# A decoder layer on one core: other places for fills, sums, evacuations and shared units, and no products of zeros in the cross attention

## The chip, the cores and the metric

One core of one Trainium2 chip runs the whole layer in one launch. The metric is the device time of that launch in microseconds (us); before the change the median of three runs is 1231.83, from 1230.77 to 1233.53. The engines are TensorE (PE, with PEld for its weight loads), VectorE (DVE), ScalarE (ACT), GpSimd (POOL) and SyncE (SP), which issues most of the transfers. All arithmetic is in float32.

## The reference

Eight sequences of 100 tokens, 512 wide, pass through one layer. Each of its three parts is added to its input, and each reads a layer norm of it:

```python
x = x + attn(layernorm(x))            # 16 query heads, 4 key heads, rotary, values 128 wide
x = x + xattn(layernorm(x), ctx)      # 16 heads of 32; ctx has 345 tokens and 16 more (DCA)
x = x + ffn(layernorm(x))             # 60 experts of 352, 4 per token, and a shared one of 1408

# xattn: queries and keys are normed per head
q = ln(x @ Wq + bq);  k = ln(y_main @ Wk + bk);  v = y_main @ Wv + bv
k_dca, v_dca = ln(y_dca @ Wk_dca + ...), y_dca @ Wv_dca + ...
ctx = softmax(q k^T) v + softmax(q k_dca^T) v_dca
return ctx @ Wo + bo
# ffn: silu(x @ gate.T) * (x @ up.T) @ down.T for the shared expert and for the four chosen ones
```

## The kernel before

The sequences are taken in four **pairs** (j = 0 and 1 in each). Before the first pair a **preamble** loads weights, centres some of them, and projects the first sequence's context, three chunks of 115 tokens, to keys and values (`FIRST_BANKS`, L783 on TensorE, L1619 and L1621 on VectorE). It also makes the keys of the 16 DCA tokens: VectorE norms them (L1609), TensorE transposes them (L788), ScalarE scales them (L1279, signal `kd_ready`).

Each engine then runs a loop over the pairs in an order that is written out by hand. A PSUM bank is handed on by semaphores: `attention_fills` lists which product fills which of the eight banks and in which order; `begin` (in `project` and the transposes) waits until the bank's former content is evacuated, `end` tells that it is full, `wait_filled` and `wait_drained` are the other side. A fill that is listed in another bank or at another place waits for another evacuation.

A pair begins with the self attention (L818 to L906). In its second half are the **ten steps** of the cross attention, `for t in range(STEPS)`: a step takes four heads of one sequence, steps 0 to 3 those of j = 0 and 4 to 7 those of j = 1, and works on three groups at once. TensorE forms the scores of group t (`four_scores`, L954, banks 0 to 3), multiplies the probabilities of group t - 2 with the values (`four_values`, L972), and transposes the probabilities of group t - 1 in three parts (`four_transposes`, L963, banks 4 and 5). VectorE takes the four maxima (`four_max`, L1771) and copies the three transposed parts (`four_T`, L1775), ScalarE does the exponentials (`four_exp`, L1340). Between them stands other work that has to be done some time:

- `STEP_HOOKS` names for each step the products that TensorE forms between the second and the third transposes, in bank 7 (6 from step 6): projections of context chunks to keys and values (`kx`, `vx`, L824; VectorE evacuates them, L1698 and L1702), the query projection `xq` and its transposes `xqT` (L842, after a norm on GpSimd, L687 to L704), the scores of the DCA tokens `ds` (L920), the transposes of their probabilities `dpT` (L928), the spread of the softmax sums `rx` (L994, from `spread_sums` on ScalarE) and the output projection `xo`.
- `STEP_ZEROS` says how often `keep_busy` multiplies zeros by zeros (L983, 128x200) before and after the third transposes. They are added to the open accumulation of the context and change nothing in it. Step 0 has two more.
- On VectorE `few(n)` puts in pieces of layer norms: in steps 1 to 4 that of the next pair's x, in steps 7 and 8 that of the third norm. `sums(j)` forms the reciprocal sums, `dca_softmax` the DCA softmax in three pieces, `residual` adds `xo` to x.

SP issues its transfers strictly in order. After the weights it writes zeros to the buffers of the routed tokens, `fill_zeros` with L464, 29 MB in nine pieces; then it enters the loop over pairs and loads the next pair's context (L430) and x (L427).

Behind the last pair the **shared expert** runs in 22 units, `shared_up(u)` (L1105): unit u is block `m = u // 2` of hidden columns for half of the tokens, `half = u % 2`. The tokens come back from DRAM transposed (`xT3`): six sequences early, the last two when the last pair is done (`xT3_loaded`). A unit from 3 on waits for the hidden product of the unit three before it (`sh_h`, L1976 on VectorE), which needs ScalarE's `silu` (L1426). Beside the units VectorE chooses experts (L1890 to L1905), whose ranks TensorE forms before unit 5 (`RANK_AT`, L1136). The routed experts follow, whose weights are loaded once the units are done.

## Time and profile before

| | us |
|---|---|
| median of three runs | 1231.83 (1230.77 to 1233.53) |
| the profiled execution | 1232.9 |
| its span, first to last instruction | 1231.1 |
| pair 0 on TensorE | from 42.08 |
| pair 1 | from 196.78, its ten steps from 271.39 to 339.51 |
| end of pair 3, first shared unit | 639.89 |
| first routed rows | 773.88 |

### The profile page before, as it was taken

What the parts mean: (1) busy time and instruction counts of PE and PEld (TensorE: products, weight loads), DVE (VectorE), ACT (ScalarE), POOL (GpSimd) and SP (SyncE); (2) the same over time, 40 slices, a digit from 0 to 9 for tenths busy, and PEclk for the clock granted to TensorE, in tenths of its full rate; (3) what the DMA queues carried; (4) which work ended last, traced back from release to release, by engine and by line L of the source; (5) the groups of instructions that cost most, each with busy time, mean ns of one, the idle gap of its engine ahead of it and who ended that gap; (6) DMA issues with size and microseconds to landing.
All of it is one profiled execution on the core that took longest, in us unless ns stands there. A gap on an engine that the chain in (4) does not pass through costs nothing.

```text
span 1231.1 us, 18953 instructions
## 1 busy us (share of the span) xinstructions
PE 1113.6 (90%) x5566; PEld 601.4 (49%) x5566; DVE 503.9 (41%) x1385; ACT 259.8 (21%) x804; POOL 369.3 (30%) x843
## 2 busy tenths in 40 slices
PE   3799889998899989999888999998888899898998
PEld 1444555445554455544554655454444445444454
DVE  7634665348554374535655711221111111121144
ACT  0142322323333332323313000111111011011100
POOL 3385451756337471574100171000000000000172
PEclk9899899999899999999998999999899899899999
DMA  8999101000010000102006592899999999999653
GB/s 313 347 397 375 36 2 54 14 12 2 2 54 14 13 1 22 39 8 92 1 27 168 178 345 75 288 383 383 383 384 380 375 385 389 388 383 381 224 139 114
DMA packets 76580, 233.06 MB, mean 189 GB/s; under 512 B 11362, under 2 KB 13766, under 8 KB 68814
## 3 DMA queue, kind: packets, MB, share of 16 engines
q1 hardware_dynamic: 58830, 197.90, 44.4%
q10 hardware_dynamic: 11520, 20.98, 4.7%
q0 software_dynamic: 6144, 13.13, 3.6%
q8 instruction: 42, 0.69, 0.2%
q14 instruction: 44, 0.36, 0.1%
HBM read 178.75 MB, written 53.22 MB: 188 GB/s over the span
## 4 chain that ended last, share of the span: by engine, by line
PE 38%; DMA 9%; issue 2%; SPq 2%; DVE 1%; ACT 0%; DVEq 0%; ACTq 0%
PE ps L1105 10%; DMA arena<-in_w 8%; PE ps L1172 7%; PE ps L1168 5%; PE ps L1266 5%; PE ps L1203 3%; PE ps L1199 3%; PE ps L824 1%; PE ps L1160 1%; PE ps L1187 1%; SPq L537 1%; PE ps L963 0%; SPq L538 0%; SPq L539 0%; PE ps L983 0%
## 5 line engine op out<-in xcount | busy, mean ns | idle before, releaser
L824 PE MATMUL ps<-arena 128*100 128x512 f32 (+3 forms) x576 | 230.3, 548 | 15.0 <-DVE arena L1742 5.5
L761 POOL DMA_INDIRECT arena<-ys_d,slot_u x32 | 36.7, 1145 | 429.6 <-issue 427.1
L824 PEld LDWEIGHTS ps<-arena 128*100 128x100 f32 (+1 forms) x576 | 88.5, 176 | 113.3 <-issue 95.9
L1172 PE MATMUL ps<-arena 128*64 128x352 f32 x640 | 115.1, 519 | 30.4 <-issue 16.2
L1105 PE MATMUL ps<-arena 128*128 128x400 f32 x352 | 122.0, 509 | 6.9 <-DMA arena<-xT_d 6.0
L1991 DVE COPY arena<-ps 128x512 f32<-128x512 f32 x40 | 27.7, 692 | 234.1 <-PE ps L1160 234.1
L906 PE MATMUL ps<-arena 128*100 128x512 f32 x256 | 114.1, 593 | 0.0
L1168 PE MATMUL ps<-arena 128*128 128x352 f32 x320 | 98.0, 459 | 0.8 <-issue 0.8
L1105 PEld LDWEIGHTS ps<-arena 128*128 128x128 f32 x352 | 67.8, 194 | 59.6 <-issue 8.7
L1340 ACT ACTIVATE arena<-ps,arena 100x345 f32<-100x345 f32 x128 | 69.4, 546 | 123.3 <-DVE arena L1771 120.4
L1172 PEld LDWEIGHTS ps<-arena 128*64 128x64 f32 x640 | 52.9, 154 | 84.9 <-issue 67.4
L687 POOL TENSOR_TENSOR arena<-arena 115x512 f32<-115x512 f32 (+1 forms) x29 | 30.2, 1041 | 181.0 <-DVE arena L1698 145.5
L1168 PEld LDWEIGHTS ps<-arena 128*128 128x128 f32 x320 | 59.2, 190 | 30.7 <-issue 1.0
L906 PEld LDWEIGHTS ps<-arena 128*100 128x100 f32 x256 | 42.3, 166 | 62.2 <-issue 58.8
L749 POOL DMA_INDIRECT xs_d<-arena,slot_u x32 | 32.7, 1022 | 124.7 <-DVE slot_u L1957 115.2
L1771 DVE TENSOR_REDUCE arena<-ps 100x1 f32<-100x345 f32 x128 | 61.9, 508 | 17.3 <-PE ps L954 17.3
L1444 ACT ACTIVATE arena<-ps 128x352 f32<-128x352 f32 x40 | 18.6, 464 | 238.1 <-PE ps L1172 145.2
L1266 PE MATMUL ps<-arena 128*128 128x400 f32 x176 | 59.5, 500 | 2.0 <-issue 2.0
L1775 DVE COPY arena<-ps 115x400 f32<-115x400 f32 x92 | 52.4, 570 | 21.5 <-PE ps L963 21.3
L963 PEld LDWEIGHTS ps<-ident,arena 100*115 100x115 f32 x384 | 49.4, 191 | 20.6 <-issue 19.6
L1203 PE MATMUL ps<-arena 128*64 128x512 f32 (+1 forms) x240 | 56.0, 601 | 0.7 <-DVE arena L2007 0.7
L690 POOL TENSOR_TENSOR arena<-arena 115x256 f32<-115x256 f32 (+3 forms) x116 | 53.5, 461 | 9.1
(222 smaller groups left out, 1488.1 us busy)
## 6 DMA issues: line engine op xcount, KB each, us to landing
arena<-in_w SPq DMA_DIRECT2D x60, 1408.0 KB, 12.4
arena<-in_w SPq DMA_DIRECT2D x60, 512.0 KB, 13.0
xs_d<-zero SPq DMA_DIRECT2D x5, 3328.0 KB, 25.5
arena<-in_w SPq DMA_DIRECT2D x60, 192.0 KB, 14.0
arena<-xs_d ACTq DMA_DIRECT2D x40, 256.0 KB, 8.0
ys_d<-arena ACTq DMA_DIRECT2D x40, 256.0 KB, 7.6
ys_d<-zero SPq DMA_DIRECT2D x2, 3328.0 KB, 24.6
arena<-in_se_up SPq DMA_DIRECT2D x11, 512.0 KB, 6.5
```

The source lines that it names most:

```text
L690: then(nc.gpsimd.tensor_tensor(s3[:, :, 0:w], s3[:, :, 0:w], s3[:, :, w:2 * w], ALU.add))
L824: last = nc.tensor.matmul(ps[0:m, k, 0:cols[1] - cols[0]], lhs(c), w[:, c, cols[0]:cols[1]], start=(c == 0), stop=(c == n_c - 1))
L906: last = nc.tensor.matmul(ps[0:S, j, :], cT[c % 2][:, g, :], w_out[:, c * G + g, :], start=(c == 0 and g == 0), stop=(c == KV - 1 and g == ...
L963: last = nc.tensor.transpose(ps[0:LC, k, r * S:(r + 1) * S], xp[(4 * t + r) % NP_][0:S, c * LC:(c + 1) * LC], ident[0:S, 0:S])
L1105: last = nc.tensor.matmul(ps[:, (u % 3) * 2 + gu, 0:400].rearrange("p (a b) -> p a b", a=4), se_w[m % 3][:, c, gu * P:(gu + 1) * P], tok, ...
L1168: last = nc.tensor.matmul(ps[:, 1 + gu, 0:I], xsT[0][:, c, :], w13_s[s][0][:, c, at:at + I], start=(c == 0), stop=(c == DC - 1))
L1172: last = nc.tensor.matmul(ps[half * HALF:(half + 1) * HALF, 3 + gu, 0:I], xsT[1][:, c, half * HALF:(half + 1) * HALF], w13_s[s][1 + half][ ...
L1203: last = nc.tensor.matmul(ps[half * HALF:(half + 1) * HALF, 7, :], hT[1][0:w, n, half * HALF:(half + 1) * HALF], w2_s[s][1 + half][0:w, n, :],
L1266: last = nc.tensor.matmul(ps[:, half * 4 + d, 0:400], w_down[:, m, d * P:(d + 1) * P], hT_all[:, m, half * 400:(half + 1) * 400], start=(m ...
L1340: nc.scalar.activation(xp[(4 * t + r) % NP_][0:S, :], ps[0:S, k, 0:LM], ACT.Exp, bias=xnm[0:S, j, h:h + 1], scale=1.0, accum_out=xsum[0:S, ...
L1771: nc.vector.tensor_reduce(xnm[0:S, j, h:h + 1], ps[0:S, k, 0:LM], AX, ALU.max, negate=True).then_inc(xmax_ready.sem, 1)
L1775: nc.vector.tensor_copy(xpT[0:LC, c, :], ps[0:LC, k, 0:4 * S]).then_inc(free[k].sem, 1)
```

## The change

Seven things are done, all in the order of the work; the products that remain are the same.

1. All products of zeros in the steps go (`STEP_ZEROS` is zero throughout, and the two in step 0 are deleted).
2. Hooks can now also stand ahead of the first transposes (`HEAD_HOOKS`) and behind the third (`TAIL_HOOKS`). `rx` of j = 0 goes to the head of step 5. `xqT` and the last key chunk go to the tail of step 3, the first value chunk to the tail of step 5, the second `dpT` to that of step 8. Banks change with them.
3. ScalarE spreads the sums of j = 0 after step 4 instead of inside step 5, and copies `rx` and `dpT` out in the other order. VectorE adds the residual `xo` of j = 0 after two maxima of step 7 instead of after four.
4. In the preamble the banks of the first projections change, the last one follows the transposes of the DCA keys, VectorE waits for `kd_ready` only behind its work on the chunks, and pair 0 starts when the first chunk is evacuated.
5. The context of pair 1 is loaded ahead of the zero fills.
6. In later pairs the next context is loaded after the last value chunk, which is now in bank 2.
7. The shared units run in the order of `UP_ORDER`: three blocks for the first half of the tokens, then these for the second half, then block by block; units 1 and 2 stand ahead of the wait for the last tokens.

```diff
+UP_ORDER = [(m, half) for half in range(2) for m in range(3)] + [(m, half) for m in range(3, MC) for half in range(2)]
...
-STEP_HOOKS = {1: [("xq", 1)], 2: [("kx", 0, 1)], 3: [("xqT", 1)], 4: [("kx", 0, 2), ("ds", 1)],
-              5: [("dpT", 0), ("rx", 0), ("vx", 0, 0)], 6: [("xo", 0)], 7: [("vx", 0, 1)], 8: [("dpT", 1)]}
-STEP_ZEROS = {1: (0, 0), 2: (0, 2), 3: (2, 3), 4: (0, 2), 5: (0, 2), 6: (0, 2), 7: (0, 2), 8: (2, 0)}
+HEAD_HOOKS = {5: [("rx", 0)]}
+STEP_HOOKS = {1: [("xq", 1)], 2: [("kx", 0, 1)], 4: [("ds", 1)], 5: [("dpT", 0)], 6: [("xo", 0)], 7: [("vx", 0, 1)]}
+TAIL_HOOKS = {3: [(("xqT", 1), 7), (("kx", 0, 2), 4)], 5: [(("vx", 0, 0), 7)], 8: [(("dpT", 1), 3), (("vx", 0, 2), 2)]}
+STEP_ZEROS = {t: (0, 0) for t in range(1, 9)}
...
-    out += [(("rx", 1), 6), (("xT3", 0), 6), (("gate", 0), 6), (("xo", 1), 0)]
+    out += [(("rx", 1), 1), (("xT3", 0), 6), (("gate", 0), 3), (("xo", 1), 0)]
...
-        FIRST_BANKS = ((2, 3, 5), (6, 7, 0))
+        FIRST_BANKS = ((2, 6, 3), (5, 7, 1))
...
             sp.dma_start(w_gate, gates.rearrange("(c p) n -> p c n", p=P)).then_inc(w_loaded["w_gate"], 16)
 
+            sp.wait_ge(first_full, 2 * LN_)
+            load_context(1, 0)
+
             sp.wait_ge(pool_pre, 7)
...
-                    sp.wait_ge(sh_up, 2 * (m - 3) + 2)
+                    sp.wait_ge(sh_up, UP_ORDER.index((m - 3, 1)) + 1)
...
-                sp.wait_ge(first_full, 2 * LN_)
-                sp.wait_ge(full[6].sem, full[6].before(i))
-                load_context(min(i + 1, PAIRS - 1), 0)
+                if i:
+                    sp.wait_ge(full[2].sem, full[2].before(i))
+                    load_context(min(i + 1, PAIRS - 1), 0)
...
             for c in range(LN_):
...
+                first_project(0, c)
+                if c < LN_ - 1:
+                    first_project(1, c)
             pe.wait_ge(dca_n, 3)
...
             last.then_inc(dca_t, 1)
+            first_project(1, LN_ - 1)
             pe.wait_ge(kd_ready, 1)
             pe.wait_ge(w_loaded["w_attn"], 16)
-            pe.wait_ge(first_free, 2 * LN_)
+            pe.wait_ge(first_free, 2)
...
+                    if j == 0:
+                        pe.wait_ge(first_free, 2 * LN_)
                     project(("k", j), S, rows, w_attn, (D, QK), DC)
...
                         transpose_x("xT2", 2, 1)
-                        keep_busy(0, 2)
...
+                    for key in HEAD_HOOKS.get(t, []):
+                        hooks[key[0]](*key[1:])
                     if 1 <= t <= FOURS:
                         four_transposes(t - 1, 0)
...
-                    if t == FOURS:
-                        context_project("vx", 0, 2)
+                    for key, _ in TAIL_HOOKS.get(t, []):
+                        hooks[key[0]](*key[1:])
...
-                m, half = u // 2, u % 2
+                m, half = UP_ORDER[u]
...
+            for u in range(1, 3):
+                shared_up(u)
             pe.wait_ge(xT3_loaded, 16 * 2)
-            for u in range(1, RANK_AT):
+            for u in range(3, RANK_AT):
                 shared_up(u)
...
                         if (t, r) == (5, 0):
-                            spread_sums(0)
-                        if (t, r) == (5, 1):
+                            spread(0)
+                        if (t, r) == (5, 2):
                             dca_T(0)
-                        if (t, r) == (5, 2):
-                            spread(0)
...
+                    if t == 4:
+                        spread_sums(0)
...
             dve.wait_ge(dca_n, 3)
-            dve.wait_ge(kd_ready, 1)
             for c in range(LN_):
...
+                    if t == 7:
+                        residual("xo", 0)
                     few(1)
...
                     if t == 7:
-                        residual("xo", 0)
                         run(pieces)
...
                     four_T(t - 1, 2)
+                    for key, _ in TAIL_HOOKS.get(t, []):
+                        if key[0] in ("kx", "vx"):
+                            (context_key if key[0] == "kx" else context_value)(*key[1:])
                     few(2)
```

Three places in the built programs show it. First SP's queue, in the preamble: what it issues after the values of the DCA tokens. Before:

```order
L457 DMA arena<-in_Wo 128x4x512
L458 DMA arena<-in_gates 128x4x61
L464 DMA xs_d<-zero 128x13x512 [waits pool_preamble]
L464 DMA xs_d<-zero 128x13x512 x4
L464 DMA xs_d<-zero 128x11x512
L464 DMA ys_d<-zero 128x13x512 x2
```

and now:

```order
L459 DMA arena<-in_Wo 128x4x512
L460 DMA arena<-in_gates 128x4x61
L432 DMA arena<-in_ctxT 128x690 [waits first_context_full]
L469 DMA xs_d<-zero 128x13x512 [waits pool_preamble]
L469 DMA xs_d<-zero 128x13x512 x4
L469 DMA xs_d<-zero 128x11x512
```

The load of the next context moved from behind all fills to ahead of them; the load of the next x stays behind.

Second TensorE in step 3, from the wait for the normed queries to the end of the step. L802 (now L810) and L419 (L421) only wait, `bank5_free` is the evacuation of bank 5. Before:

```order
L802 REGISTER_ALU [waits heads_normed]
L842 MATMUL ps<-ident,arena 128x100 [waits bank7_free]
L842 MATMUL ps<-ident,arena 128x100 x3
L983 MATMUL ps<-zero 128x200 x2
L802 REGISTER_ALU
L963 MATMUL ps<-ident,arena 115x100 [waits bank5_free]
L963 MATMUL ps<-ident,arena 115x100 x3
L983 MATMUL ps<-zero 128x200 x3
```

and now:

```order
L973 MATMUL ps<-ident,arena 115x100 [waits bank5_free]
L973 MATMUL ps<-ident,arena 115x100 x3
L810 REGISTER_ALU [waits heads_normed]
L850 MATMUL ps<-ident,arena 128x100 [waits bank7_free]
L850 MATMUL ps<-ident,arena 128x100 x3
L832 MATMUL ps<-arena 115x512 [waits bank4_free]
L832 MATMUL ps<-arena 115x512
```

The third transposes (L963, now L973) moved ahead of the transposed queries (L842, now L850), the zeros are gone, and the last key chunk (L832) came from step 4.

Third TensorE in step 5, from the second transposes on. Before:

```order
L963 MATMUL ps<-ident,arena 115x100 [waits bank4_free]
L963 MATMUL ps<-ident,arena 115x100 x3
L802 REGISTER_ALU [waits dca_probs_ready]
L928 MATMUL ps<-ident,arena 128x100 [waits bank7_free]
L928 MATMUL ps<-ident,arena 128x100
L802 REGISTER_ALU [waits spread_sums_ready]
L994 MATMUL ps<-ident,arena 128x100 [waits bank7_free]
L994 MATMUL ps<-ident,arena 128x100 x3
L802 REGISTER_ALU
L824 MATMUL ps<-arena 115x512 [waits bank7_free]
L824 MATMUL ps<-arena 115x512
```

and now, from the products with the values of group 3 on:

```order
L982 MATMUL ps<-arena 32x100 x3
L810 REGISTER_ALU [waits spread_sums_ready]
L1004 MATMUL ps<-ident,arena 128x100 [waits bank7_free]
L1004 MATMUL ps<-ident,arena 128x100 x3
L973 MATMUL ps<-ident,arena 115x100 [waits bank3_free,bank2_free,bank5_free,bank1_free,bank0_free]
L973 MATMUL ps<-ident,arena 115x100 x3
L973 MATMUL ps<-ident,arena 115x100 [waits bank4_free]
L973 MATMUL ps<-ident,arena 115x100 x3
L810 REGISTER_ALU [waits dca_probs_ready]
L938 MATMUL ps<-ident,arena 128x100 [waits bank7_free]
```

The spread of the sums (L994, now L1004) moved from behind `dpT` (L928, now L938) to ahead of the first transposes; the value chunk (L824) now follows the third ones.

## Rows read from the trace of the kernel before

**Rows 1.** The page: share of TensorE, and one of its costliest groups (ScalarE).

```profile
PE 1113.6 (90%) x5566; PEld 601.4 (49%) x5566; DVE 503.9 (41%) x1385; ACT 259.8 (21%) x804; POOL 369.3 (30%) x843
...
L1340 ACT ACTIVATE arena<-ps,arena 100x345 f32<-100x345 f32 x128 | 69.4, 546 | 123.3 <-DVE arena L1771 120.4
```

**Rows 2.** Groups by form, TensorE: count | busy us, mean ns | idle before.

```profile
L983 PE MATMUL ps<-zero 128*128 128x200 f32 x152 | 35.8, 364 | 0.0
```

**Rows 3.** Timeline of TensorE in the steps of pair 1.

```profile
276.71 0.86 PE L983 MATMUL ps<-zero 128*128 128x200 f32 x4
...
293.19 0.56 PE L842 MATMUL ps<-ident,arena 100*128 100x100 f32 x4 [1.44 <-POOL arena L704]
...
295.67 1.88 PE L983 MATMUL ps<-zero 128*128 128x200 f32 x6
...
299.79 1.89 PE L824 MATMUL ps<-arena 128*115 128x512 f32 x4
...
308.89 0.56 PE L994 MATMUL ps<-ident,arena 100*128 100x100 f32 x4 [1.80 <-ACT arena L1303]
310.05 3.17 PE L824 MATMUL ps<-arena 128*115 128x512 f32 x4 [0.59 <-ACT arena L1303]
...
315.60 0.84 PE L954 MATMUL ps<-arena 32*100 32x345 f32 x8
...
323.39 0.84 PE L954 MATMUL ps<-arena 32*100 32x345 f32 x8
...
327.24 3.29 PE L824 MATMUL ps<-arena 128*115 128x512 f32 x4 [1.37 <-DVE arena L1742]
```

**Rows 4.** Timeline of VectorE in the steps of pair 1.

```profile
282.80 0.69 DVE L1707 TENSOR_TENSOR arena<-ps,arena 100x512 f32<-100x512 f32 x1 [0.70 <-PE ps L824]
...
292.65 0.56 DVE L1775 COPY arena<-ps 115x400 f32<-115x400 f32 x1
...
295.91 0.57 DVE L1775 COPY arena<-ps 115x400 f32<-115x400 f32 x1 [0.84 <-PE ps L963]
...
298.33 0.94 DVE L1771 TENSOR_REDUCE arena<-ps 100x1 f32<-100x345 f32 x2 [1.59 <-PE ps L954]
...
302.33 1.04 DVE L1544 TENSOR_TENSOR arena<-arena 100x1 f32<-100x1 f32 x1
...
306.38 1.35 DVE L1771 TENSOR_REDUCE arena<-ps 100x1 f32<-100x345 f32 x3
...
316.45 0.94 DVE L1771 TENSOR_REDUCE arena<-ps 100x1 f32<-100x345 f32 x2 [1.87 <-PE ps L954]
```

**Rows 5.** Busy time by stretch, the ten steps of pair 1; behind POOL the granted clock.

```profile
271.39:339.51 68.12, 60.58 (x483) 38.15 (x483) 48.34 (x139) 23.86 (x75) 31.34 (x89) 0.92 0.02 7
```

**Rows 6.** Timeline of VectorE, preamble and step 1 of pair 0.

```profile
36.99 0.69 DVE L1619 TENSOR_TENSOR arena<-ps,arena 115x512 f32<-115x512 f32 x1 [3.75 <-ACT arena L1279]
...
132.37 0.68 DVE L1553 BATCH_NORM_STATS2 arena<-arena 100x6 f32<-100x512 f32 x1
```

**Rows 7.** Timeline of TensorE, start of pair 0 and its step 0.

```profile
42.08 1.59 PE L818 MATMUL ps<-ident,arena 100*128 100x100 f32 x8 [6.72 <-DVEq L1622]
...
125.96 3.38 PE L824 MATMUL ps<-arena 128*115 128x512 f32 x4 [3.42 <-DMA arena<-in_ctxT]
```

**Rows 8.** Timeline of SP's queue, pair 0: last fills and the context behind them.

```profile
84.04 24.64 SPq L464 DMA_DIRECT2D ys_d<-zero  x3
108.80 6.62 SPq L430 DMA_DIRECT2D arena<-in_ctxT  x1
```

**Rows 9.** Timeline of ScalarE, step 5 of pair 1.

```profile
308.51 0.33 ACT L1303 ACTIVATE arena<-ps 128x200 f32<-128x200 f32 x1
```

**Rows 10.** Timeline of TensorE, the first shared units.

```profile
639.89 5.64 PE L1105 MATMUL ps<-arena 128*128 128x400 f32 x16 [0.87 <-DVE arena L1742]
...
653.37 24.44 PE L1105 MATMUL ps<-arena 128*128 128x400 f32 x64 [5.98 <-DMA arena<-xT_d]
```

**Rows 11.** Timeline of VectorE, its first hidden product of the shared units.

```profile
663.87 0.57 DVE L1976 TENSOR_TENSOR arena<-arena,ps 128x400 f32<-128x400 f32 x1 [2.96 <-ACT arena L1426]
```

25 lines of the change are left out of this document (12 added, 13 removed).

## The prediction, made before the changed kernel ran

> **What bounds the kernel now.** I read the page first: TensorE is busy for 90% of the span [rows 1], so time on its path is what counts. The groups by form then show products of `zero` alone [rows 2]: 76 matmuls (each is two records), 35.8 us, in steps 0 to 8 of the cross attention, 19 in each pair. They can go, but the time follows only where TensorE itself is late. So I read TensorE's instructions of pair 1 in order of time [rows 3]: the largest stalls in its ten steps are 1.44 (for the norm of queries on GpSimd), 1.80 and 0.59 (for ScalarE's copies out of bank 7) and 1.37 (for VectorE's residual); with three of 0.8 they come to 7.5 us. VectorE in the same stretch [rows 4] has no wait between those at 282.80 and 295.91, so steps 2 and 3 are its own. Last comes the clock [rows 5]: the steps take 68.1 us at a mean of 0.92. The loss stands in [rows 3]: a projection of keys takes 1.89, but 3.17 and 3.29 behind the stalls, not far from the half rate of 1.2 GHz. Of 68.1 us some 47 are work at full clock: less 7.5 of stalls, 8.2 of zeros (19 at 0.43, as two take 0.86 [rows 3]) and 5.4 that the clock takes (8%).
>
> **The head.** VectorE stands 3.75 us for ScalarE's keys of the short context before it touches the first chunks [rows 6], and TensorE stands 6.72 until all six are evacuated [rows 7]. Now VectorE begins 3.75 earlier and pair 0 asks for the first chunk alone, so it starts between 3.75 and 6.72 earlier. The context for pair 1, 345 KB, goes out ahead of the zero fills, so the wait of 3.42 and the slow projection behind it (3.38 for 1.89) [rows 7] go as well. That adds up to some 9 to 12 us, 11 with a start 6 earlier, but I do not count it. SP is shut in the fills until 108.80 [rows 8], and the next x is still behind them: with the context moved ahead the same bytes stand in front of it. The context landed at 125.96 [rows 7]; I take 126.3 for x. VectorE started the norm that needs it at 132.37 [rows 6]. So the head gives 6.0, and the rest turns into a wait for x; between 5 and 7, as x lands at 127.4 or 125.4.
>
> **Steps 0 to 3.** The zeros ahead of step 1 go, so the query projection is evacuated 0.8 earlier (VectorE waited 0.70 for it [rows 4]), and its unbroken chain moves by that. TensorE, with no zeros, comes to the third transposes of step 3 at about 290.3 and stands some 2.0 us for the copy that before starts at 292.65 [rows 4]: longer than the 1.44 that it replaces. Behind it stand the transposed queries and now also the last key chunk, moved here from step 4, which VectorE must evacuate before its first maximum of step 4. At full clock that maximum comes at 296.5 instead of 298.33 [rows 4], 1.8 less; with the chunk at half the clock (3.4 instead of 1.7), 0.2 less. I take 0.7, nearer the slow end: behind the stall of 1.44 three products of zeros took 1.88, where two took 0.86 before [rows 3].
>
> **Steps 4 and 5.** From that maximum to the first of step 6 it is 18.1 us before (298.33 to 316.45 [rows 4]). Step 4 on VectorE, 8.05 to 306.38, loses the evacuation of the key chunk (0.7), the waits around it (0.6) and most of an instruction of 1.04 that takes 0.16 elsewhere (0.7) [rows 4]: 6.05. The spread of the sums (`rx`) moves ahead of the transposes, but its bank 7 is free only when VectorE has read the scores of the short context at that step's end: TensorE stands 1.9 us there, in place of the 1.80 later on. Then a maximum and an exponential (0.5 and 0.6 [rows 1]), the spread's copy (0.5), two exponentials (1.1) and the `dpT` copy (0.33 [rows 9]) free bank 7 for the value chunk: 3.1. Chunk 1.8, products of the short context 1.0, first scores 0.3: 12.3 in all, 5.8 less. If the clock falls behind the stall, the chunk and what stands around it take up to 2.3 longer: 3.5 less. I take 4.8, as the work between stall and chunk uses up most of a slow stretch.
>
> **Step 6** runs without a stall from 315.60 to 323.39 [rows 3]; only its zeros go: 0.9 (0.8 to 0.9).
>
> **Steps 7 to 9** take 16.1 us before (323.39 [rows 3] to the end at 339.51 [rows 5]). The residual now follows the second maximum, so the wait of 1.37 goes, and the slow chunk of 3.29 with it. VectorE then bounds them. By [rows 4] two maxima take 0.9, a copy 0.5, an evacuation 0.7, a piece of a norm 0.2: counted from the scores, first maximum at 1.0, residual done at 2.5, maximum, copy and maximum to 3.9, pieces and second copy to 5.2, chunk 5.8, third copy 6.7, sums 8.05, next copy 8.6. TensorE stands 1.6 for the third copy and 0.75 for the last; its chunk and spread end at 11.3, the norm that the next transposes need at 13.5: 13.6, so 2.5 less. With the last chunk at half the clock 0.8 less. I take 1.1, near the slow end, for two stalls close together.
>
> **Shared units.** Units 1 and 2 now need the early tokens alone and fill the stall of 5.98 ahead of 653.37 [rows 10]. But unit 3 waits for the first hidden product, which VectorE starts at 663.87, late itself behind router and activation tables [rows 11]. With 5.5 a unit [rows 10] TensorE stands from 658.4 to 664.5 and begins slowly, as it does now: four units took 24.44 where 22 would do. Unit 4 ends at about 677.6 either way: 0, between 2.2 less (no slow start) and 0.5 more. The later weight loads wait for unit 3 instead of 1, but two more units and the ranks stand ahead of their use. Everything behind is shifted whole.
>
> **Sum.** A pair saves 0.7 + 4.8 + 0.9 + 1.1 = 7.5 (5.3 to 11.0), four of them 30, the head 6: 36.0 less. The profiled execution took 1232.9 us, so 1196.9; the median is 1.1 lower: **1196**. The bounds together: 7 + 44 + 2.2 less gives 1179, 5 + 21.2 - 0.5 gives 1206.
>
> **Rivals.** (1) *Slower: the clock.* The zeros hold the engine busy; without them the steps could run by turns at 1.2 and 2.4 GHz. With half of the 47 us at 1.2 GHz the work takes 70.5, and with some 5 of stalls 7.4 more than 68.1; four pairs less the head make 24 more, 1256; with no stalls left 1236. It decides once more than 27% of the work runs slow: 47 x 1.27 and 10 of stalls are 68.1 plus the 1.5 of head for each pair. For it: the slow projections of pair 1 stand behind stalls of 1.4 to 2.4 us, and I expect new ones of 1.6 to 2.0. Against: slow stretches ended while TensorE had work, and slow work fills stalls. Chance 0.08.
> The Trainium skill, "TensorE: Matmul & The Clock Gate", section "A second HAM failure mode: psum-queue depth-cycling", says that short idle times between groups of matmuls, as PSUM banks are cycled, can make the clock swing between its levels; it speaks against this change, and by it the time would be this rival's. The trace agrees that it happens (a mean of 0.92 [rows 5]), not that it goes on.
> (2) *Small gain.* Each stall brings a slow stretch that falls on the chunk VectorE waits for, and the head gives less: 2 to 5 a pair, 1207 to 1223, around 1214. Chance 0.14.
> (3) *x lands early.* Then the head gives its 11: 1191. Against it: the context, right ahead of x in the queue, came at 125.96 [rows 7]. Chance 0.10.
> (4) *Nothing measurable.* Zeros and moves only change places with stalls, within 0.2% (2.5 us, about what a measurement can tell): 0.03.
> My forecast has 0.65.
>
> **Range and chances.** 1178 to 1212 holds the forecast's bounds, rival 3 and a third of rival 2. Faster 0.65 + 0.10 + 0.14 = 0.89, same 0.03, slower 0.08.
>
> **What would show it.** No products of zeros by 200 columns. Pair 0 starts 4 to 6 us earlier, and VectorE waits for x until about 126. The steps take near 60 us, with stalls of about 2 us ahead of the third transposes of step 3 and ahead of the spread in step 5, both for VectorE, and none for GpSimd's norm. From the end of the last pair to the ranks the distance is unchanged, with a stall of about 6 us ahead of unit 3. The mean clock of the steps tells the rivals apart: 0.85 to 0.93 is mine, under 0.8 the first. I am wrong if the steps shrink by more than 11 or less than 5 us, or if x does not hold pair 0.

## The result, and the profile after

The changed kernel takes 1221.74 us (median of 20 runs, 1209.33 to 1233.12) beside 1229.34 for the kernel before (20 runs, 1223.70 to 1234.19). The ratio is 0.9915, 95% interval 0.9892 to 0.9938. It counts the 14 runs that lie within 1.5% of the fastest, while the medians of all 20 give 0.9938. Measured a second time the changed kernel took 1228.23 beside 1230.65, a ratio of 0.9977 (0.9947 to 1.0007). So by the medians it is 7.6 and 2.4 us faster, and the second interval takes in no difference as well; 36 were forecast, and both medians lie above the forecast's range of 1178 to 1212. The first profiled execution was the longest of those 20 runs; the rows below are from one of the second measurement, 1223.36 us (span 1221.5).

TensorE's busy share has not moved against [rows 1]; the page says:

```profile
PE 1099.5 (90%) x5414; PEld 583.7 (48%) x5414; DVE 505.9 (41%) x1385; ACT 260.8 (21%) x804; POOL 368.1 (30%) x843
```

The busy time by stretch (columns as in [rows 5]; behind the granted clock stand the busy share of the DMA engines and what they moved, in GB/s): self attention of pair 0; its steps up to pair 1; the ten steps of pair 1; from the first routed products to the end.

```profile
36.40:113.01 76.61, 74.24 (x328) 36.73 (x328) 37.02 (x92) 23.53 (x88) 49.93 (x119) 1.00 1.04 376
113.01:191.65 78.64, 65.35 (x466) 36.44 (x465) 49.07 (x140) 24.89 (x77) 31.00 (x89) 0.85 0.21 70
...
266.32:330.35 64.03, 56.25 (x445) 33.41 (x444) 48.43 (x139) 24.16 (x75) 31.30 (x89) 0.89 0.03 7
...
756.40:1221.40 465.00, 418.62 (x1804) 218.33 (x1804) 101.09 (x239) 46.45 (x88) 34.07 (x32) 0.95 0.91 327
```

The steps of pair 1 take 64.0 us instead of 68.1 [rows 5], at a granted clock of 0.89 instead of 0.92; pair 0 from its steps on runs at 0.85. Where the slow work lies is seen in the timeline of TensorE in pair 1, which answers to [rows 3] (a transpose shows as one record, so x12 in L973 are twelve):

```profile
287.55 1.09 PE L973 MATMUL ps<-ident,arena 100*115 100x100 f32 x4 [1.84 <-DVE arena L1788]
288.43 0.87 PE L850 MATMUL ps<-ident,arena 100*128 100x100 f32 x4
289.10 2.79 PE L832 MATMUL ps<-arena 128*115 128x512 f32 x4
...
300.37 0.56 PE L1004 MATMUL ps<-ident,arena 100*128 100x100 f32 x4 [1.84 <-DVE arena L1764]
...
303.15 2.65 PE L832 MATMUL ps<-arena 128*115 128x512 f32 x4
...
306.60 0.84 PE L964 MATMUL ps<-arena 32*100 32x345 f32 x8
...
313.69 0.84 PE L964 MATMUL ps<-arena 32*100 32x345 f32 x8
...
316.76 1.97 PE L832 MATMUL ps<-arena 128*115 128x512 f32 x4 [0.60 <-DVE arena L1755]
...
320.97 0.38 PE L982 MATMUL ps<-arena 115*32 115x100 f32 x8 [1.01 <-DVE arena L1788]
321.52 2.73 PE L973 MATMUL ps<-ident,arena 100*115 100x100 f32 x12 [0.17 <-issue]
324.05 0.54 PE L938 MATMUL ps<-ident,arena 100*128 100x100 f32 x2
324.38 3.65 PE L832 MATMUL ps<-arena 128*115 128x512 f32 x4
327.82 0.82 PE L1004 MATMUL ps<-ident,arena 100*128 100x100 f32 x4
...
330.70 0.56 PE L826 MATMUL ps<-ident,arena 100*128 100x100 f32 x4 [0.35 <-DVE arena L1577]
```

The predicted stalls are there: 1.84 ahead of the third transposes of step 3 and 1.84 ahead of the spread in step 5, both for VectorE. Behind each the next chunk is slow: 2.79 and 2.65, where one at full clock takes 1.89 [rows 3]. The worst comes in step 8. Stalls of 0.60 (in step 7) and 1.01 (in step 8) come first, and all of step 8 from its transposes on runs at half the clock: its chunk takes 3.65.

VectorE in the same pair, which answers to [rows 4]: first maximum of step 4, two small instructions of step 4's norm, first maximum of step 6.

```profile
292.94 0.94 DVE L1784 TENSOR_REDUCE arena<-ps 100x1 f32<-100x345 f32 x2
...
296.02 0.60 DVE L1557 TENSOR_TENSOR arena<-arena 100x1 f32<-100x1 f32 x1
296.66 0.96 DVE L1560 SCALAR_TENSOR_TENSOR arena<-arena 100x1 f32<-100x1 f32 x1
...
307.46 0.94 DVE L1784 TENSOR_REDUCE arena<-ps 100x1 f32<-100x345 f32 x2 [0.93 <-PE ps L964]
```

In pair 0 VectorE now stands for x, and TensorE behind it; the answer to [rows 6], and TensorE's row:

```profile
126.73 0.69 DVE L1566 BATCH_NORM_STATS2 arena<-arena 100x6 f32<-100x512 f32 x1 [6.10 <-DMA arena<-in_x]
...
128.38 1.10 PE L973 MATMUL ps<-ident,arena 100*115 100x100 f32 x4 [4.69 <-DVE arena L1788]
```

The queue of SP, which answers to [rows 8], shows why x comes then: SP issues it only when it gets out of the three fills of the results.

```profile
84.77 24.74 SPq L469 DMA_DIRECT2D ys_d<-zero  x3
109.63 8.47 SPq L429 DMA_DIRECT2D arena<-in_x  x2
```

Pair by pair, from the first transposes of x to those of the next pair: pair 0 now 155.3 (154.7 before), though it starts 5.7 earlier; pair 1 144.6 (148.1); pair 2 143.4 (147.5). The first routed products start at 756.40 instead of 775.37, 19.0 earlier. From there to the end, in what is called the routed stretch below, it is 465.1 us instead of 455.8, with the same code: 9.3 are gone again. In the first profiled execution, the one of 1233.12 us, the first routed products started at 761.70, 13.7 earlier than before, and the stretch took 469.7.

### The profile page after: what moved, and what is told of

The parts are those of the page before. It is cut to its first block, busy times and chain, and to the rows that moved or that the text cites. A ratio compares the mean times of both kernels' runs of the same rounds, so it can differ in the third digit from the quotient of the medians.

```text
span 1231.3 us, 18523 instructions
## 1 busy us (share of the span) xinstructions
PE 1107.0 (90%) x5414; PEld 588.4 (48%) x5414; DVE 506.1 (41%) x1385; ACT 261.5 (21%) x804; POOL 372.9 (30%) x843
## 4 chain that ended last, share of the span: by engine, by line
PE 64%; DMA 12%; SPq 8%; DVE 8%; issue 6%; ACT 1%; DVEq 0%; ACTq 0%
PE ps L832 14%; DMA arena<-in_w 9%; PE ps L1116 9%; PE ps L916 7%; PE ps L1185 7%; PE ps L1181 5%; SPq L469 5%; PE ps L1279 5%; PE ps L1216 3%; PE ps L1212 3%; PE ps L973 2%; PE ps L905 1%; DMA arena<-in_x 1%; DVE arena L1784 1%; DVE arena L1788 1%
## 5 line engine op out<-in xcount | busy, mean ns | idle before, releaser
L832 PE MATMUL ps<-arena 128*100 128x512 f32 (+3 forms) x576 | 233.3, 553 | 7.6 <-ACT arena L1301 3.7
L1185 PE MATMUL ps<-arena 128*64 128x352 f32 x640 | 119.6, 535 | 39.6 <-issue 31.9
L832 PEld LDWEIGHTS ps<-arena 128*100 128x100 f32 (+1 forms) x576 | 91.1, 181 | 107.3 <-issue 95.4
L1185 PEld LDWEIGHTS ps<-arena 128*64 128x64 f32 x640 | 56.5, 158 | 95.2 <-issue 70.1
L1116 PEld LDWEIGHTS ps<-arena 128*128 128x128 f32 x352 | 67.7, 194 | 60.1 <-issue 9.1
L1181 PEld LDWEIGHTS ps<-arena 128*128 128x128 f32 x320 | 59.2, 190 | 30.7 <-issue 1.0
L973 PE MATMUL ps<-ident,arena 100*115 100x100 f32 x384 | 59.3, 297 | 16.0 <-DVE arena L1788 15.4
L973 PEld LDWEIGHTS ps<-ident,arena 100*115 100x115 f32 x384 | 51.1, 202 | 32.1 <-DVE arena L1788 19.5
```

What stands on the lines that cost most here:

```text
L832: last = nc.tensor.matmul(ps[0:m, k, 0:cols[1] - cols[0]], lhs(c), w[:, c, cols[0]:cols[1]], start=(c == 0), stop=(c == n_c - 1))
L973: last = nc.tensor.transpose(ps[0:LC, k, r * S:(r + 1) * S], xp[(4 * t + r) % NP_][0:S, c * LC:(c + 1) * LC], ident[0:S, 0:S])
L1116: last = nc.tensor.matmul(ps[:, (u % 3) * 2 + gu, 0:400].rearrange("p (a b) -> p a b", a=4), se_w[m % 3][:, c, gu * P:(gu + 1) * P], tok, ...
L1181: last = nc.tensor.matmul(ps[:, 1 + gu, 0:I], xsT[0][:, c, :], w13_s[s][0][:, c, at:at + I], start=(c == 0), stop=(c == DC - 1))
L1185: last = nc.tensor.matmul(ps[half * HALF:(half + 1) * HALF, 3 + gu, 0:I], xsT[1][:, c, half * HALF:(half + 1) * HALF], w13_s[s][1 + half][ ...
```

## The experiments

### The clock: zeros back, zeros alone, zeros only in the stalls

**after_again, before_again.** Both kernels once more, unchanged, for the spread of their stretches.

> The changed kernel once more. Two things of its first profile are in question: the routed experts took 471.1 us from their first weights to the end (457.2 before), and the pairs gained 2 to 4 us each. If the transfer rate of the routed weights differs from execution to execution, with no tie to the change, that stretch is anything between 445 and 470 here, longer where its rate in GB/s is lower. If starting it earlier makes it longer, it is 471 within 3 again. The pairs should repeat within 2 us each: pair 1 144.6, pair 2 145.7, pair 3 138.7 from the first transposes of x to those of the next pair.

> The kernel before once more, for the spread of its stretches: if the transfer rate of the routed weights varies from execution to execution, its routed stretch is not 455.8 us at 383 GB/s again but anywhere from 450 to 465, longer at a lower rate; the pairs repeat to 1 us (148, 147.5, 142).

Measured: the changed kernel 1228.23 us (10 runs), pairs 1 and 2 at 144.6 and 143.4, routed stretch 465.1 at 375 GB/s. The kernel before in a single run 1225.94, pairs 1 and 2 at 147.2 and 146.8, stretch 447.9 at 392 GB/s (455.8 at 383 in the first profile). The stretch moves with its transfer rate.

The pairs repeat less well than expected: pairs 1 and 2 to within 2.4 us, but pair 3 of the changed kernel, from its first transposes to the ranks, took 182.2 in the first profile and 179.1 in the second, and pair 0 of the kernel before 154.7 and 157.7. before_padded and before_light (below) run the code of the kernel before up to the routed experts too, and after_light that of the changed one. By the means of these four and three executions the change gains 0.9 us in pair 0, 2.8 in pair 1 and 2.5 in pair 2, and the first routed products start 16.6 earlier (from 774.3 to 776.2 before, from 756.4 to 761.7 now). The first profile of the kernel before, by which the prediction was made, has the shortest pair 0 and the longest pairs 1 and 2 of its four.

**all_zeros** (the diff is against the changed kernel, as below where nothing else is said):

```
-STEP_ZEROS = {t: (0, 0) for t in range(1, 9)}
+STEP_ZEROS = {1: (0, 0), 2: (0, 2), 3: (2, 3), 4: (0, 2), 5: (0, 2), 6: (0, 2), 7: (0, 2), 8: (2, 0)}
...
                         transpose_x("xT2", 2, 1)
+                        keep_busy(0, 2)
```

> The changed kernel with all 19 products of zeros a pair put back where they stood, two of them in step 0. Theory A (the clock): without them TensorE falls to half its clock behind each stall, and the work behind it pays. Then step 8 of pair 1 runs at the full clock (12 transposes 1.6 us instead of 2.74, the last value chunk 1.9 instead of 3.65), steps 7 to 9 take 15 instead of 17.0; against that stand up to 0.43 for each of the zeros that does not fall into a stall, some 10 of them, 4 a pair: time the same within 0.5%, granted clock of the ten steps 0.93 to 0.97 instead of 0.89. Theory B (VectorE bounds the steps, the clock of TensorE only fills its waits): the zeros cost their 8.2 us a pair less what lies in stalls (4), so 4 us a pair, 16 in all, 1.3% slower than the changed kernel, equal to the kernel before or slower.

Measured: 1218.44 us, 0.9916 of before (0.9886 to 0.9946), where the kernel without zeros had 0.9977 on the same chip and 0.9915 in the first measurement: the time does not tell the two apart, the steps have to. The steps of pair 1 take 63.5 us, at a clock of 0.95. Step 8 in TensorE's timeline:

```profile
320.24 0.38 PE L982 MATMUL ps<-arena 115*32 115x100 f32 x8 [0.66 <-DVE arena L1789]
320.75 1.02 PE L973 MATMUL ps<-ident,arena 100*115 100x100 f32 x8
321.61 0.87 PE L993 MATMUL ps<-zero 128*128 128x200 f32 x4
322.31 0.55 PE L973 MATMUL ps<-ident,arena 100*115 100x100 f32 x4
322.70 0.34 PE L938 MATMUL ps<-ident,arena 100*128 100x100 f32 x2
322.88 1.90 PE L832 MATMUL ps<-arena 128*115 128x512 f32 x4
```

The chunk takes 1.90 instead of 3.65. Theory A holds for the steps, theory B (16 us slower) falls: 19 products of zeros a pair cost nothing, the first routed products even start 1.9 us earlier (754.5) than in after_again. The rest of the difference between the two profiles lies in the routed stretch, 452.1 us at 389 GB/s in this one.

**stall_zeros:**

```
-STEP_ZEROS = {t: (0, 0) for t in range(1, 9)}
+STEP_ZEROS = {t: (0, 0) for t in range(1, 9)} | {3: (4, 0), 4: (0, 2), 7: (0, 2)}
...
+                    if t == 5:
+                        keep_busy(0, 4)
                     for key in HEAD_HOOKS.get(t, []):
```

> The changed kernel with 12 products of zeros a pair, only where TensorE stands: 4 ahead of the third transposes of step 3 (1.85 us of waiting), 2 at the end of step 4 (0.93), 4 ahead of the spread in step 5 (1.84), 2 at the end of step 7 (1.01). Theory A (the clock): the chunks of keys and values behind them take 1.9 instead of 2.6 to 3.65, step 8 runs at the full clock; 0.7 in step 3, 0.7 in step 5, 1.5 to 3 in steps 7 to 9: 3 to 4.5 a pair, 12 to 18 us in all, 0.978 to 0.982 of the kernel before. Theory B (VectorE bounds the steps): the zeros lie in waits and change nothing, time that of the changed kernel within 0.3%.

Measured: 1214.06 us, 0.9863 of before (0.9799 to 0.9926; 4 runs), the steps of pairs 1 to 3 at 60.8, 60.9 and 59.2 us, clock 0.97. Step 3 of pair 1:

```profile
281.74 1.54 PE L993 MATMUL ps<-zero 128*128 128x200 f32 x8
283.74 0.65 PE L973 MATMUL ps<-ident,arena 100*115 100x100 f32 x4 [0.47 <-DVE arena L1790]
284.23 0.51 PE L850 MATMUL ps<-ident,arena 100*128 100x100 f32 x4
284.96 1.97 PE L832 MATMUL ps<-arena 128*115 128x512 f32 x4 [0.23 <-DVE arena L1790]
```

The zeros lie in the stall and cost nothing; the chunk takes 1.97 instead of 2.79. The steps gain 3.8, 3.2, 1.9 and 1.2 us in pairs 0 to 3 against after_again: theory A, at two thirds of the size forecast. Two places are left. In step 5 of pair 1 a stall of 1.12 remained behind the zeros, and the value chunk still took 3.62. And behind the steps of pairs 1 and 2 the clock falls now: between them and the next pair it is 0.78, where it was 1.00 in after_again, and the projections there take 6.05 in pair 1, where they took 4.36 in the kernel before. First the two rows of step 5, then the projections here and in the kernel before:

```profile
295.33 0.56 PE L1004 MATMUL ps<-ident,arena 100*128 100x100 f32 x4 [1.12 <-DVE arena L1766]
...
298.11 3.62 PE L832 MATMUL ps<-arena 128*115 128x512 f32 x4 [0.37 <-ACT arena L1318]
...
325.10 6.05 PE L832 MATMUL ps<-arena 128*100 128x61 f32 x16 [0.59 <-ACT arena L1303]
```

```profile
340.71 4.36 PE L824 MATMUL ps<-arena 128*100 128x61 f32 x16 [0.69 <-ACT arena L1288]
```

So counted from pair to pair the gain is only 3.1, 1.5 and 0.2 us in pairs 0 to 2, and the first routed products start 4.7 earlier than in after_again (751.70), not 10.

**before_no_zeros** (against the kernel before): both lines of all_zeros the other way round.

> The kernel before with its products of zeros left out and nothing moved: the zeros alone. Theory A (the clock): the 8.2 us of zeros a pair kept the clock up; where VectorE and ScalarE are waited for anyway, the stalls grow and more of the chunks run at half the clock: 0 to 2 us a pair less than before, 0 to 0.7% faster, clock of the ten steps 0.86 to 0.90. Theory B (TensorE simply had 8.2 us too much to do): 4 to 5 us a pair less, 1.3 to 1.6% faster.

Measured: 0.9996 of before (0.9964 to 1.0028), no difference. In the profile the first routed products start 6.7 us earlier; the steps of pair 1 take 65.6 us, 2.7 less, at a clock of 0.92, though steps 4 and 5 take 20.6 from scores to scores where they took 18.1. That lies between the theories; three other executions with the code of the kernel before took 66.0 to 67.3, and against those it is 0.4 to 1.7 less, which agrees with A, as the time does.

The kernels together, ten steps of pairs 1, 2 and 3 (from the first scores to the end of the last product of the short context):

| kernel | zeros a pair | steps, us | clock, pair 1 |
|---|---|---|---|
| before | 19 | 68.3 67.7 66.7 | 0.93 |
| before_no_zeros | 0 | 65.6 64.8 63.8 | 0.92 |
| all_zeros (moves alone) | 19 | 63.5 62.5 59.2 | 0.95 |
| changed (after_again) | 0 | 64.0 62.8 60.5 | 0.89 |
| stall_zeros | 12 | 60.8 60.9 59.2 | 0.97 |
| stall_zeros_early_x | 14 | 59.1 59.1 59.8 | 1.00 |

By this table, with the old order, taking the zeros out saves 2.8 us in the steps of a pair; with the moves made, it costs 0.7; the moves themselves save 5.8. One row is one execution, and those of one kernel differ: over the three pairs the changed kernel took 64.2 us a pair on average in its first profile and 62.4 in the second. By the means of the four executions of the kernel before and the three of the changed one the figures are 2.2, 1.3 and 5.2. So the moves clearly shorten the steps, and the cost of leaving all zeros out is small beside that spread.

### The head: what holds x

**early_x:**

```
-            fills_started += fill_zeros(ys_d, TILES, TILES + NOV)
-            assert fills_started == ZERO_FILLS
...
                     load_context(i + 1, 1)
+                    if i == 0:
+                        fills_started += fill_zeros(ys_d, TILES, TILES + NOV)
+                        assert fills_started == ZERO_FILLS
```

> The changed kernel with the three zero fills of the results (9.2 MB) put behind the loads of x and of the second context, nothing else: the order of SP's queue alone. Theory X (the fills in flight hold x): x lands some 10 us earlier, TensorE's wait of 6.4 us in pair 0 goes with the slow clock behind it, pair 0 is 7 to 10 us shorter than 79.0, the other pairs stay as they are (144.6, 145.7, 138.7); 7 to 10 us less than the changed kernel. The rest of the gain of the combined kernel over that with the zeros in the stalls alone then comes from the two more products of zeros. Rival: the gain came from those zeros, pair 0 stays within 2 us.

Measured: 1214.26 us, 0.9895 of before (0.9866 to 0.9925). SP's queue:

```profile
43.81 41.31 SPq L469 DMA_DIRECT2D xs_d<-zero  x6
85.24 8.13 SPq L429 DMA_DIRECT2D arena<-in_x  x2
115.73 0.36 SPq L432 DMA_DIRECT2D arena<-in_ctxT  x1
116.13 12.80 SPq L469 DMA_DIRECT2D ys_d<-zero  x3
```

x goes out 24 us earlier, right behind the fills ahead of it, so its own waits were over by then, and pair 0 takes 144.9 us instead of 155.3: 10.4 less, with pairs 1 and 2 as they were (144.1, 143.8). Theory X holds, a little above its upper end; the time is 7.5 and 14.0 us under the two medians of the changed kernel.

**stall_zeros_early_x:** both diffs in one, with `keep_busy(0, 6)` in step 5.

> The kernel with zeros in the stalls (4 in step 3, 2 in step 4, here 6 ahead of the spread of step 5, 2 in step 7) and, in pair 0, the three zero fills of the results (9.2 MB) put behind the loads of x and of the second context. If the fills in flight hold x, it lands at about 115 to 118 instead of 127.5, TensorE's wait of 6.4 us for VectorE's copy goes and the slow clock behind it: pair 0 is 6 to 10 us shorter than 79.0. If x has another cause (its own wait for the first residual at 111), less than 2. The 2 more products of zeros in step 5 cover the wait of 1.12 that was left there and bring the value chunk of 3.62 to 1.9: 1 to 2 us in pairs 1 and 2. Together 7 to 13 us less than with the zeros in the stalls alone, which is 0.973 to 0.981 of before.

Measured: **1195.31 us (1194.1 to 1196.4, 4 runs), 0.9712 of before (0.9679 to 0.9745)**, faster than both kernels, a little better than expected. The value chunk of step 5 in pair 1, with the zeros, the stall that is left, and the granted clock of the ten steps by stretch:

```profile
281.89 2.30 PE L994 MATMUL ps<-zero 128*128 128x200 f32 x12
284.65 0.56 PE L1005 MATMUL ps<-ident,arena 100*128 100x100 f32 x4 [0.46 <-DVE arena L1767]
...
287.43 1.97 PE L833 MATMUL ps<-arena 128*115 128x512 f32 x4 [0.38 <-ACT arena L1319]
```

```profile
251.87:310.98 59.11, 54.92 (x473) 33.70 (x472) 47.97 (x139) 24.18 (x75) 31.50 (x89) 1.00 0.03 8
```

early_x is the same kernel without the 14 products of zeros, and that makes it the clearest test of them: 1214.26 us without, 1195.31 with them, and the intervals against before do not touch. Of the 20.0 us between the two profiles 13.2 come ahead of the routed experts (746.77 and 733.60), where the clock in the steps of pair 1 is 0.89 and 1.00; the rest lies in the routed stretch, at 375 and 381 GB/s.

### The shared units

**units_undone:** `UP_ORDER` plain, all units but the first behind `xT3_loaded`.

> The changed kernel with the shared units in their old order and the wait for the last tokens ahead of unit 1 again. Theory of the prediction: the order is worth nothing, as the wait only moves to the first hidden product; from the end of the last pair to the ranks 43 to 44 us, as with it (43.47) and before (42.98). Rival: the new order is worth one of the two waits, 2 us or more. If it also had a part in the slower routed stretch of the changed kernel, the median would fall by 8.

Measured: 1224.66 us (1221.05 to 1228.53). From the last product of the steps to the ranks 43.96 us, with the new order 43.95. It is worth nothing, as predicted.

### The routed stretch: what takes 9 us back

**after_light, before_light.** From the third round on SP loads only the down weights:

```
+            def reload(s, b, at):
...
+                rows = w2[e, 0:256, :].rearrange("(p c) n -> p c n", c=2)
+                for c in range(2):
+                    sp.dma_start(w2_s[s][b][:, c:c + 1, :], rows[:, c:c + 1, :]).then_inc(w_ready[s][b], 16)
...
-                    load_single(s, ii * 2 + (s + 2))
+                    reload(s, 0, ii * 2 + (s + 2))
...
```

The gate and up products then run on the weights that lie there, which leaves out what the later experts would need: these two kernels are for timing alone.

> The changed kernel with the routed rounds relieved of most of their transfers: from the third round on the gate and up weights (1408 KB of 2112 KB an expert) are not loaded, the products run on those that lie there; only the down weights are loaded, in three pieces. The rounds are then bound by TensorE (17.7 us of work a round), not by the transfers, and what stands ahead of them is unchanged. To be compared with the same edit of the kernel before. Theory R (what the change earned ahead of the routed experts was given back by the transfers of the weights alone): 13.7 to 19 us less than the light kernel before, as the first routed products started 13.7 and 19.0 us earlier in the two profiles, with a narrow spread of runs (some 6 us), as against 24 us in the full kernel. Theory P (the pairs themselves vary and gain less than those two profiles show): 7 us less, and a spread as wide as in the full kernel.

> The kernel before with the same edit: from the third round on no gate and up weights are loaded. By both theories faster than the full kernel before, by up to 20 rounds x (19.6 - 17.7) = 38 us; it is the yardstick of the light changed kernel. If the spread of the full kernel comes from the transfer rate, its runs lie within 4 us.

Measured: 1169.61 us (1168.9 to 1173.1) and 1186.74 (1183.8 to 1189.4): 17.1 less. The stretch takes 410.06 us in the one and 410.08 in the other. The first routed products start at 757.97 in the one and 775.34 in the other, 17.4 apart. So all that is earned ahead of the routed experts arrives when the transfers do not bound them, and the four runs of each lie within 4.2 and 5.6 us (20 runs of the changed kernel: 23.8). Theory R holds.

The rate by stretch, 310 us of the routed rounds from 20 us behind their first products (last column GB/s); the kernel before, the changed one, the light changed one:

```profile
795.37:1105.37 310.00, 283.33 (x1281) 144.23 (x1280) 57.63 (x160) 33.97 (x64) 0.00 (x0) 0.94 1.02 383
```

```profile
776.40:1086.40 310.00, 279.07 (x1259) 142.01 (x1258) 56.35 (x156) 33.33 (x63) 0.00 (x0) 0.94 1.02 375
```

```profile
777.97:1087.97 310.00, 310.00 (x1491) 157.59 (x1491) 66.64 (x185) 39.27 (x74) 0.00 (x0) 1.00 0.57 184
```

In the full kernels the transfers fill the stretch (a share of 1.02) at 383 or 375 GB/s. The next runs ask what sets that rate.

**after_delayed:** 38 products of zeros ahead of `shared_up(0)`.

> The changed kernel with 38 products of zeros (16.5 us by 0.43 each) on TensorE after the last pair, ahead of the first shared unit, so that everything behind starts about when it does in the kernel before. If the length of the routed stretch has nothing to do with when it starts, the time is that of the changed kernel plus 14 to 16.5: some 1238 to 1243, slower than before. If an earlier start itself makes the stretch longer, the rate of its transfers rises from 371-375 to 383 GB/s, the stretch falls from 465-470 to 456, and the time is some 1226 to 1231, that of the kernel before.

Measured: 1234.99 us (1223.7 to 1245.8), between the two forecasts, and so is the stretch with 461.4 at 379 GB/s. Inconclusive.

**before_padded:** `xs_d` longer by 5 tiles, in the kernel before.

> The kernel before with 5 more tiles of rows (1.25 MB) at the end of the buffer of the routed rows, never used: the buffer of the results, and what lies behind it, stands at other addresses. If the place of the buffers in memory sets the transfer rate of the routed stretch, the median moves by over 4 us one way or the other (the changed kernels give up 7 to 9 in that stretch). If not, it stays within 2 us of the kernel before.

Measured: 1228.91 us, 1.0007 of before (0.9983 to 1.0032), stretch 453.9 at 384 GB/s. That change of addresses makes no difference.

**head_undone, head_only.** The parts of the diff at `FIRST_BANKS`, `first_project`, `first_free`, `kd_ready` and the early `load_context(1, 0)`, taken out of the changed kernel, and put alone into the kernel before.

> The changed kernel with the head of the kernel before: the old banks of the first chunks, the old waits ahead of pair 0, and the context of pair 1 behind the zero fills again; steps and units as changed. Two questions. Ahead of the routed experts: pair 0 starts at 42.1 instead of 35.4 to 36.4, the wait of 3.4 us for the context comes back and that for x goes; the first routed products start 3 to 7 us later than in the changed kernel (761.7, 756.4). In the routed stretch: if the head is what makes its transfers slower, the median falls back to 453 us there, and the kernel comes to some 1217 to 1220, faster than the changed one in spite of its late start; if not (the steps, or no part of the change), the stretch stays at 460 to 468 and the time is 1228 to 1234.

> The kernel before with the head of the changed one alone: banks of the first chunks, waits ahead of pair 0, the context of pair 1 ahead of the zero fills; steps, zeros and units as before. By the prediction pair 0 starts 6 us earlier and the rest of the head turns into a wait for x: the first routed products start 4 to 7 us earlier than in the kernel before (775.4). If the head makes the routed transfers slower, the routed stretch is 460 to 468 and the time 1231 to 1238; if not, the stretch is 448 to 457 and the time 1222 to 1226.

Measured: head_undone 1217.44 us, 0.9934 (0.9903 to 0.9964), start 761.9, stretch 457.8 at 383 GB/s; head_only 1228.07, 1.0009 (0.9971 to 1.0047), start 767.7, 465.4 at 376 GB/s. The two stretches point to the head. The times do so less: the interval of head_undone overlaps those of the changed kernel, and head_only stays below the 1231 to 1238 that was expected of a slower stretch.

**context_late, before_context_early, best_context_late.** The one transfer of the context moved behind the fills in the changed kernel, ahead of them in the kernel before, and between the two groups of fills in the fastest kernel.

> The changed kernel with the context of pair 1 back behind the zero fills, nothing else: the order of one transfer of 345 KB. Up to the routed experts: TensorE in pair 0 waits for the context again, as in the kernel before, and the first routed products start at 756 to 764. If the place of this transfer goes with the slower routed transfers, the stretch takes 453 us at the median (383 GB/s or more), and the time is 1211 to 1219. If it is another part of the head, it takes 460 to 468, and the time is 1219 to 1232.

> The kernel before with the context of pair 1 ahead of the zero fills, nothing else. The wait of 3.4 us for the context turns into one for x: the first routed products start at 772 to 776. If the place of this transfer makes the routed transfers slower, the stretch takes 460 to 468 us and the time is 1234 to 1244, slower than before; if not, it takes 448 to 457, and the time is 1223 to 1231.

> The combined kernel (zeros in the stalls, the fills of the results behind x) with the context of pair 1 between the two groups of fills, ahead of x. The context lands near 100, before pair 0 asks for it at 113, and x soon after 111, so nothing changes ahead of the routed experts (first products near 733.6). If the early place of the context makes the routed transfers slower, the stretch falls from 459 to 453 and the time from 1195 to about 1189; if not, it stays at 1194 to 1197.

Measured: context_late 1229.45 us, 1.0007 (0.9983 to 1.0032), stretch 458.7 at 381 GB/s in its profile; before_context_early 1229.84, 0.9992 (0.9960 to 1.0023), start 765.8, stretch 462.0 at 377; best_context_late 1199.31 (1194.6 to 1209.8), stretch 467.1 at 374. Putting the context back did not make the changed kernel or the fastest one faster, so its place is not the cause, or not alone.

What is shown: over 17 profiled executions of full kernels the stretch ran from 447.9 us at 392 GB/s to 469.7 at 371, longer where the rate was lower. What stays open is why the rate differs. Most kernels that come to the stretch earlier have the lower rate, but all_zeros, 21 us early, had 389, and the kernel before differs by 9 GB/s between two executions.

## Why the prediction was wrong

Three steps failed: counting pair 0 as a pair like the others ("four of them 30"), the term for steps 7 to 9 with its price of a slow stretch, and "everything behind is shifted whole". Of the 36.0 us forecast, 9.6 are left between the two profiles compared here. Missing are 8.4 in the head and pair 0, 4.0, 3.3 and 1.4 in pairs 1 to 3, and 9.3 in the routed stretch.

**The head, 6.0: right.** Pair 0 starts at 36.40 instead of 42.08, and VectorE's norm that needs x at 126.73 instead of 132.37 [rows 6]; I had x at 126.3. But the 7.5 that pair 0 should have earned on top did not come: it ends 5.1 earlier than before (191.65 for 196.78; in the three other executions of that code it ended at 199.2 to 200.0). **This step failed**: I took it for a pair like the others, and it has the long wait for x in its steps, with a clock of 0.85 behind it. early_x gives the size: 10.4.

**Steps 0 to 3, 0.7: 0.3.** From the first scores of pair 1 to the first maximum of step 4 it is 26.62 us (292.94 less 266.32); before 26.94, by [rows 4] and the start of [rows 5]. The stall was 1.84 (2.0 forecast), the chunk 2.79. Within the bounds.

**Steps 4 and 5, 4.8: 3.6.** From there to the first maximum of step 6, 14.52 instead of 18.12. That is near the bound for a slow chunk (3.5), and it is slow, 2.65. One part of the term was wrong in kind: the instruction of 1.04 [rows 4] was to shrink to 0.16. Now two of that norm take 0.60 and 0.96. GpSimd works beside them (its timeline in pair 1):

```profile
295.56 1.04 POOL L709 TENSOR_TENSOR arena<-arena 115x512 f32<-115x512 f32 x1
296.57 1.04 POOL L692 TENSOR_TENSOR arena<-arena 115x512 f32<-115x512 f32 x1
```

In pair 3, where GpSimd has no next context to norm, the same two on VectorE take 0.15 and 0.16:

```profile
584.10 0.15 DVE L1557 TENSOR_TENSOR arena<-arena 100x1 f32<-100x1 f32 x1
584.28 0.16 DVE L1560 SCALAR_TENSOR_TENSOR arena<-arena 100x1 f32<-100x1 f32 x1
```

The Trainium skill, "SBUF — State Buffer", section "Who interferes with whom", says that an instruction of VectorE with two inputs in SBUF contends with one of GpSimd that reads there, the later one standing until the first is done. The trace agrees with it by these durations, and by where they end: in this trace 20 of the norm's one-column instructions (lines 1554, 1557 and 1560) take over 0.25 us, and each ends within 0.1 us of the end of a GpSimd instruction. No run took GpSimd's work away from pair 1.

**Step 6, 0.9: 0.7**, 7.09 from scores to scores instead of 7.79, a little below its bounds of 0.8 to 0.9.

**Steps 7 to 9, 1.1 less: 0.9 more. This step failed.** From the scores of step 7 to the transposes behind the steps 17.01 us (313.69 to 330.70) instead of 16.12. I had let "the last chunk at half the clock" cost 1.7 of the 2.5 gained. But all of step 8 from its transposes on runs slow: 12 transposes 2.73 instead of about 1.6, the chunk 3.65 instead of 1.9, the spread 0.82 instead of 0.51. all_zeros shows the step at full clock, and there steps 7 to 9 take 13.85 us, 3.2 less, close to the 13.6 that the prediction had for full clock. So the moves there were priced rightly; the bound for the clock had been worked out for one slow instruction, where a slow stretch takes all that lies in it.

So pairs 1 and 2 give 3.5 and 4.2 by these two profiles (2.8 and 2.5 by the means above) where 7.5 was forecast: in the steps the second rival was right, 2 to 5 a pair, by the mechanism it named. That 1221.74 lies in its range (1207 to 1223) is in part luck, as the range held no loss in the routed stretch, and the second measurement, 1228.23, lies outside. The steps of pair 1 shrank by 4.1 us, less than the 5 below which the prediction called itself wrong, while their mean clock of 0.89 lies in the 0.85 to 0.93 that it gave for itself. The first rival, slower by the clock, did not come about. The page that it drew on, "TensorE: Matmul & The Clock Gate" of the Trainium skill, section "A second HAM failure mode: psum-queue depth-cycling", names what the rows show, a clock that falls behind short stalls. Here that took back about half of the gain in the steps of pair 1: from 68.1 us they came to 64.0, and with 14 products of zeros in the stalls to 59.1.

**Shared units, 0: right**, with the stall ahead of unit 3 as forecast, for VectorE's hidden product:

```profile
646.46 12.39 PE L1116 MATMUL ps<-arena 128*128 128x400 f32 x32 [5.88 <-DVE arena L1993]
```

**"Everything behind is shifted whole": this step failed too.** Of the 19.0 us at the first routed products 9.3 were taken back by the routed stretch, whose transfers ran at 375 GB/s instead of 383. The light kernels show that the products are shifted whole (17.1 us) and the transfers are not. The prediction never asked what bounds that stretch: a DMA share of 1.02 stood in the trace of before. None of my rivals held this mechanism. Why the rate was lower stays open.

The sum: 36.0 forecast; 5.1 by the end of pair 0, 3.5, 4.2, and 6.1 from the start of pair 3 to the ranks make 18.9 ahead of the routed experts, then 9.3 lost. stall_zeros_early_x takes 1195.3, close to the forecast 1196; that is chance, as it is another kernel with two more edits, but it shows that the moves pay once the clock is kept up and x comes early.

## What to carry to other kernels

A product of zeros costs nothing where it lies in a stall and may keep the clock of the work behind it: before taking such fillers out, find the stalls that will open, and leave the fillers there. Judge them by the distance from pair to pair, not by the steps alone, as a slow stretch can move behind what is measured. Where a slow stretch is to be priced, count all the instructions that lie in it, not the one that is waited for. A gain ahead of a stretch that is bound by transfers is not certain to come through it, so look at the DMA share of what lies behind before writing "shifted whole"; and a small load that is due soon goes ahead of large fills that nobody waits for yet.

## What the hardware showed that was not expected

The granted clock fell behind stalls as short as 0.60 and 1.01 us close together, and cost more than the stalls: step 8 lost over 3 us to 1.6 of standing. With 14 products of zeros in the stalls the steps of pair 1 ran at 1.00, in the same kernel without them (early_x) at 0.89.

The rate of the routed weights ran from 371 to 392 GB/s, 6% apart, over kernels whose code in that stretch is the same, and the stretch from 469.7 to 447.9 us with it. Within one kernel the two executions were 383 and 392 (before), and 371 and 375 (changed).
